# TensorE's step with the relative-value matmuls ahead of the shift

## The reference

```
content  = einsum('bhqd,bhkd->bhqk', q, k)
relative = einsum('bhqd,qkd->bhqk', q, rel_k[idx])
w        = softmax((content + relative) / sqrt(8), axis=-1)
out      = einsum('bhqk,bhkd->bhqd', w, v) + einsum('bhqk,qkd->bhqd', w, rel_v[idx])
```

## Time and profile before

| what | value |
|---|---|
| median of three runs | 470.05 us |
| the profiled execution | 470.23 us |
| its span, first to last instruction | 468.4 us |
| TensorE busy (matmuls) | 418.0 us, 89% |
| VectorE busy | 407.1 us, 87% |
| ScalarE busy | 416.4 us, 89% |
| GpSimd busy | 314.1 us, 67% |
| mean granted TensorE clock | 0.983 |

### The profile page before, as it was taken

The page is one execution under the profiler, slowest core; times in us unless marked ns, Lnnn a source line. Parts: engine busy times, 40 slices in busy tenths (PEclk is TensorE's granted clock), DMA queues, the critical chain, the costliest instruction groups (busy, mean ns, idle before and its releaser), DMA issues.

```text
span 468.4 us, 24907 instructions
## 1 busy us (share of the span) xinstructions
PE 418.0 (89%) x10258; PEld 337.8 (72%) x10258; DVE 407.1 (87%) x887; ACT 416.4 (89%) x806; POOL 314.1 (67%) x370
## 2 busy tenths in 40 slices
PE   0888888689999999999999999999999999999863
PEld 0345554477888888888888888888788888788753
DVE  8879766549999999999999999999999999999875
ACT  2889999459999999999999999999999999999810
POOL 6557777616675767687776868786778777686520
PEclk9999999889999999999999999999999999999987
DMA  7624745963112525424252524242543515244786
GB/s 160 216 65 121 128 90 133 164 134 79 27 37 57 75 59 85 83 68 78 61 94 47 86 48 83 60 71 62 93 76 64 96 36 94 50 85 92 152 184 186
DMA packets 159529, 43.09 MB, mean 92 GB/s; under 512 B 122321, under 2 KB 156601, under 8 KB 159289
## 3 DMA queue, kind: packets, MB, share of 16 engines
q1 hardware_dynamic: 152304, 40.19, 41.9%
q10 hardware_dynamic: 7112, 1.31, 1.8%
HBM read 21.55 MB, written 16.79 MB: 82 GB/s over the span
## 4 chain that ended last, share of the span: by engine, by line
PE 52%; issue 12%; ACT 9%; DVE 6%; POOL 0%; ACTq 0%; DVEq 0%; POOLq 0%
PE ps_s L1031 10%; PE ps_s L1026 10%; PE ps_s L1133 10%; PE ps_o L1048 9%; PE ps_t L1118 7%; DVE mx L1243 5%; PE ps_r L1072 5%; ACT xr L1169 4%; ACT big L1204 4%; PE ps_s L1108 1%; ACT p L1184 1%; PE ps_r L252 1%; DVE big L1247 1%; POOL big L872 0%; ACT ps_y L1184 0%
## 5 line engine op out<-in xcount | busy, mean ns | idle before, releaser
L872 POOL TENSOR_TENSOR big<-p,big 128x512 f16<-128x512 f32 x128 | 148.6, 1161 | 102.8 <-ACT big L1204 102.1
L1031 PE MATMUL ps_s<-by_q_room,e 96*128 96x64 f16 x2048 | 103.2, 192 | 0.0
L1026 PE MATMUL ps_s<-qbd,kst 96*128 96x128 f16 x1024 | 99.5, 219 | 2.9 <-PEq L300 2.5
L1247 DVE TENSOR_TENSOR big<-ps_y,big 128x512 f16<-128x512 f32 x128 | 88.1, 688 | 15.6 <-ACT big L1204 13.9
L1287 DVE TENSOR_REDUCE mcol<-ps_t 128x4 bf16<-128x512 bf16 x128 | 87.6, 684 | 9.9 <-PE ps_t L1118 5.9
L1243 DVE TENSOR_TENSOR mx<-s,ps_s 128x512 bf16<-128x512 bf16 x128 | 86.7, 677 | 3.2 <-ACT s L1162 2.1
L1162 ACT ACTIVATE s<-ps_s 128x512 bf16<-128x512 f32 x128 | 80.3, 627 | 5.9 <-PE ps_s L1031 5.9
L1031 PEld LDWEIGHTS ps_s<-by_q_room,e 96*128 96x128 f16 x2048 | 85.4, 97 | 0.1
L1204 ACT ACTIVATE big<-p 128x512 f16<-128x512 f32 x128 | 84.7, 662 | 0.0
L1184 ACT ACTIVATE ps_y<-ps_s 128x512 f32<-128x512 f32 x128 | 76.0, 594 | 8.7 <-PE ps_s L1133 4.7
L276 POOL COPY by_q_room<-qrel 96x256 uint32<-96x256 uint32 x128 | 78.5, 630 | 3.4 <-POOLq L300 3.1
(11 more groups left out here) (110 smaller groups left out, 530.8 us busy)
## 6 DMA issues: line engine op xcount, KB each, us to landing
rel_dram<-xr SPq DMA_DIRECT2D x32, 256.0 KB, 3.3
xr<-rel_dram SPq DMA_DIRECT2D x60, 128.0 KB, 3.6
kst<-big SPq DMA_DIRECT2D x48, 64.0 KB, 2.0
qrel<-qr_dram SPq DMA_DIRECT2D x192, 16.0 KB
qbd<-q_dram SPq DMA_DIRECT2D x192, 16.0 KB
y_dram<-big SPq DMA_DIRECT2D x4, 512.0 KB, 2.9
big<-y_dram SPq DMA_DIRECT2D x4, 512.0 KB, 5.8
out<-big SPq DMA_DIRECT2D x8, 256.0 KB, 3.2
```

Source lines behind the costliest of these rows:

```text
L872: nc.gpsimd.tensor_tensor(probs[:, k // 8, 1, 1, k % 8, :], p32[:, k % 2, 1, :], probs[:, k // 8, 0, 1, k % 8, :], ALU.subtract).then_inc( ...
L1026: nc.tensor.matmul(bank[:, P * g:P * g + P], kst[:, g, S * k + P * kh:S * k + P * kh + P], rhs, start=(g == 0), stop=False, skip_group_che ...
L1031: ins = nc.tensor.matmul(bank.rearrange("p (h q j) -> p h q j", q=Q0, j=J)[:, :, q, :], e4[:, first:first + P], rhs.rearrange("p (h j) -> ...
L1247: nc.vector.tensor_tensor(probs[:, k // 8, 1, 0, k % 8, :], ps_y[:, :], probs[:, k // 8, 0, 0, k % 8, :], ALU.subtract).then_inc(lo0_ready, 1)
```

## The change

In `body` of TensorE the call `relative_step(qb, k)` moves from behind the shift to ahead of the wait for `mcol_ready`, so that it follows `pv` directly. No instruction is added or removed, and no other engine's list changes.

```diff
                     if unit(qb, k - 3):
                         pv(*unit(qb, k - 3))
 
+                    relative_step(qb, k)
                     pe.wait_ge(mcol_ready, n + 1)
                     for kh in range(KH):
                         for g in range(G):
                             ins = nc.tensor.matmul(ps_s[:, k % 2, kh, P * g:P * g + P],
                                                    mcol[:, k % 2, g:g + 1].to_broadcast([P, P]), negid[:, :],
                                                    start=False, stop=(g == G - 1), skip_group_check=True)
                         ins.then_inc((shifted0, shifted)[kh], 1)
-                    relative_step(qb, k)
```

## The result

The changed kernel takes 489.81 us (median of four runs, 489.22 to 490.64) against 471.02 beside it: ratio 1.0404, interval 1.0379 to 1.043. It is slower by 19 us; the prediction was 490. The profiled execution took 490.14 us with a span of 488.3.

The account below looks back on a forecast made before the run. A closed loop from shift to shift through ScalarE's exponentials was taken to bound the kernel. 85 steps cost 17.9 us more, 27 with copies 0.8, four with two relative parts 1.0: 19.7 on 470.2 gives 490, range 483 to 500.

Parts of the forecast that it names:

- The step with and without relative matmuls: TensorE before the change: 68 matmuls take 2.59 us, 83 take 2.62, so sixteen more cost next to nothing.
- The shift 0.23 later: On TensorE the shift would start 0.68 us behind the first value matmul instead of 0.45.
- the first rival: The extra time of a matmul width change returns between value and relative matmuls (32, 24 columns): 499.6 us; chance 0.12.
- The plain step, 2.82: A step without a copy of the relative sums takes 2.82 us from shift to shift, against 2.61 on average before.
- The long step, 2.98: A step with a copy of the relative sums takes 2.98 us, against 2.95 before; 27 of them add 0.8.
- the four double ones: Steps 121 to 124, with two relative parts each, take 3.04 us each, 12.2 together against 11.2 before.
- The transposes 0.1 late and harmless: TensorE's transposes come 0.1 us late, waiting for the maximum; the following scores wait for half 0's exponential anyway.
- two seams saved: Two of four changes between full-width and 32-column matmuls vanish per step, saving 0.20 us of TensorE issue time.
- The second rival, 483: The path over the elementwise maximum, not the wait for the exponentials, sets the steps: 483 us; chance 0.06.
- The third, faster: With over 0.23 us of slack in the scores' wait, plain steps fall to 2.48: 459 us; chance 0.04.
- The fourth, the clock: TensorE idles and its clock falls to 1.2 GHz in a tenth of the loop, adding over 10 us; chance 0.01.
- The waits to be seen: TensorE idle about 0.3 us ahead of half 0's scores, some 37 us over the loop; ScalarE waiting for the shift.

## Why the prediction was right, point by point

- *What bounds.* Right. TensorE was not the bound though its records covered 97% of the loop: taking 8 of 16 relative matmuls away gave nothing, and taking them out of the changed kernel gave 9 us.
- *The step with and without relative matmuls.* The conclusion was right, that sixteen matmuls more cost nothing, but the comparison was worse than it need be. The counts of 68 and 83 take in matmuls that straddle the stretch's ends; 60 and 76 start in these steps. And the 0.03 between 2.59 and 2.62 is not theirs: the step just before, also without relative matmuls, takes 2.62 (114.32 to 116.94 in the earlier trace rows), and with them steps of 2.62 and 2.59 alternate as well.
- *The shift 0.23 later.* Right: 0.68 behind the first value matmul (267.61 to 268.29) instead of 0.45. The first relative matmul follows at +0.35, so between value and relative matmuls no seam comes back; the first rival (499.6) falls with it.
- *The plain step, 2.82.* Measured 2.84 in the mean: two alternating lengths, 2.81 and 2.85. *The long step, 2.98.* Most are 2.96, their mean 2.99. The 112 steps were to take 321.5 us and took 321.9; the four double ones 12.2 and took 12.3. What lies outside was put at 0 and came to -0.7 ahead of shift 8 (118.81 against 119.53) and +0.4 behind shift 124 (35.3 against 34.9), and the stray steps, left as they were, happened to be nearly as costly as before. That the total is right to 0.2 us is in that part luck.
- *The transposes 0.1 late and harmless.* Right: they start at 266.01, 0.54 behind the shift instead of 0.45, when the maximum (265.28, 0.68 long) has ended, and a maximum made later by 0.08 left the plain steps alone. What I called two seams saved is shown for one only: at the other place, shift to transposes, this wait covers whatever a seam would be, so no run here tells.
- *The second rival, 483.* It named a path that is real, but in the changed kernel it holds only in long steps. That path decides in the kernel with the relative matmuls behind the transposes.
- *The third, faster.* It hung on slack over 0.23 us. There was none to speak of, as every group ahead of the shift was paid in full.
- *The fourth, the clock.* It was granted at 1.00 in both stretches, with TensorE's records on 295.9 of 321.9 us in the first.
- *The waits to be seen.* The mechanism was right and the size off: I expected some 37 us of idle TensorE ahead of line 1026, and the page has 17.4 us, 7.7 of them put down to the exponential. A matmul's record lasts 0.22 us while the next would start after 0.06, so each wait is shortened in the records by the length of the record before it. Of the 0.53 us between transposes and scores at 266.01, with four transposes to issue in some 0.23, no idle is marked at all.

## What to carry to other kernels

Where several engines look 85 to 90% busy, add up one step's closed loop (the chain of waits that leads from an instruction back to the same one a step later) from the starts of instructions, with the short times from one engine's signal to the next one's start, and compare it with the step. In this kernel work placed in TensorE's one gap is free, and the same work a few lines further up is paid in full. Before moving a block of work ahead of a signal, ask who waits for the signal and what the engine will do in the gap that the block leaves. The reverse is a way to gain: give the signal earlier (here the shift ahead of the value matmuls), until the next loop closes.

## What was not expected of the hardware

- ScalarE's records overlap: activations of 128x512 last 0.58 to 0.65 us and follow each other at 0.48 to 0.49 (265.91 and 266.40 in the changed kernel). Five of them need some 2.4 us of a 2.84 us step, yet the records cover 299.9 of the 321.9 us: a busy share of 93% hides waits.
- On VectorE the order of three small instructions moved the step: masking, reciprocal, sum to the column maxima start 0.21, 0.46 and 0.14 apart (0.81 in all), reciprocal, masking, sum 0.47, 0.26 and 0.20 apart (0.93). Of the 0.12 that the order costs, 0.05 lies between the masking and what follows it, where the sum has to wait for the masking's result, and 0.06 behind the sum; what causes the latter no run shows.
- A change from 32-column to full-width matmuls costs about 0.10 us (0.16 from the start of the last value group to the shift, 0.058 from group to group; 0.16 also from the last relative group to the shift of the changed kernel); between 32-column and 24-column ones nothing: the last value group and the first relative one follow at the spacing within them (six spacings in 0.35, 267.61 to 267.96).
